# A two-layer graph kernel on one core: the last fix-up stage without its carry, products moved from GpSimd to ScalarE, and normalised rows dealt differently

## The chip, the cores and the metric

The kernel runs on one NeuronCore of one Trainium2 chip. The metric is device time in microseconds; 1742.92 us is the median of three runs of the kernel before. Engines are named as in the profile: PE is TensorE (PEld its weight loads), DVE is VectorE, ACT is ScalarE, POOL is GpSimd, SP is SyncE, which here only issues DMAs.

## What is computed

There are N = 100000 nodes with 128 features, and E = 25000 edges sorted by destination. Cut to what matters:

```python
# layer 0: attention over the edges that end in a node, then residual and layer norm
x = layernorm(x + gnn0(x, edge_attr, edge_index))
# layer 1
X1   = x @ w2
msgs = X1[src] * edge_weight[:, None]
agg  = segment_sum(msgs, dst, num_segments=N)
x    = layernorm(x + relu(x @ w1 + agg + b))
```

Only some 25000 nodes are the end of an edge. So both layers are computed twice: a dense pass over all nodes as if there were no edges, and a fix-up pass that computes the nodes with edges properly and scatters their rows over the dense ones.

## The kernel before

**Tiles.** Nodes are handled in G = 196 groups of 512 rows (128 partitions x NJ = 4 rows). Edges lie in a grid of 128 partitions x T = 196 columns, in order of destination; partition p holds edges p*196 to p*196+195. A run is a stretch of edges with the same destination. A run's sum is formed along the columns of a partition; where a run goes over from one partition to the next, the sum so far has to be carried across.

**Stages, in order of time.** (A) Dense layer 0 over 196 groups, with the gathers and the attention logits of all edges: until about 657 us. (B1) Fix-up of layer 0, 98 steps of two edge columns, scattered to `h_tab` by POOL, with the dense layer 1 of the first G1 = 49 groups between them: from about 715 to 1065 us. (D2) The dense layer 1 of groups 49 to 195: to about 1383 us. (C) Fix-up of layer 1, T4 = 49 quads of four edge columns: to the end.

**Stage D2.** For each group ACT copies the transposed rows out of PSUM (`d2_evict`, L817), PE multiplies (L619), DVE adds and takes the statistics (`d2_relu` L1238, `pair_stats` L992), ACT computes the reciprocal deviation (`inv_std`, L682 and L684), and the four rows of the group are normalised: three by ACT (`scale_rows`, L728, NZ = 3), one by DVE (`normalise`, L1002). SP loads each group ahead, ACT's queue stores it. Beside this POOL gathers the source rows of one edge column at a time from `h_tab` (L499), and four columns later multiplies them with the edge weights (L505, `agg_b2`); a gather waits for the product of six columns before. DVE forms the run sums (`run_sum`, L1228), one column after the other, some six columns behind.

**Stage C.** Per quad k: SP loads the four columns' own rows (`xg<-hd_scr`, L383); PE transposes them and the four run sums (L653, L656; signal `t_c`); ACT copies both out of PSUM (`c_evict`, L863 and L864, after `t_c` of its quad and `mm_c` of the quad two before); PE forms the product (L667, L671, L672; signal `mm_c`). DVE waits for `mm_c`, adds the carried sum `carg` to each of the four rows where the run began in an earlier partition (L1314), then normalises the quad before (L1002; signal `z_c`), then adds the residual (L1329) and takes statistics (L992). ACT's `inv_std` of quad k-3 stands ahead of its `c_evict(k)`. POOL waits for `z_c` and issues four scatters of 128 rows to the output (L514). DVE may write a buffer of normalised rows again when its scatters have landed; there are U = 4 such buffers. `carg` is made ahead of the loop: `last_sums` (L1279, L1280), two transposes (L639, L640), a scan (L1298), a product (L644), a copy (L1301).

The order of the work on each engine is the order of the program; every wait is a semaphore.

## Time and profile before

| | |
|---|---|
| median of three runs | 1742.92 us (1738.02 to 1744.43) |
| span of the profiled execution, first to last instruction | 1705.3 us |
| PE, PEld, DVE, ACT, POOL busy over the span | 73%, 64%, 79%, 72%, 61% |
| share of the chain that ended last, by engine | ACT 36%, DVE 29%, PE 9%; "another core or an unknown queue" 9%, "issue" 11% |
| HBM traffic over the span | 230 GB/s |

For the profiled execution only its span is given, no time of its own around it; the median of the runs is 37.6 us over the span. "Remote" or "another core or an unknown queue" in a row means that the profile found no releaser for the wait; on one core it is a signal whose sender the records don't show. A row of the timeline gives start, duration, engine, line, operation, tiles, count, and in brackets the idle time before it with its releaser.

### The profile page before, as it was taken

The numbers are of one execution on the slowest core, as the hardware profiler recorded it, in microseconds if no ns is written. First come the engines' busy times: TensorE is split into PE (matmuls) and PEld (weight loads), VectorE is DVE, ScalarE is ACT, GpSimd is POOL, SyncE is SP. The second block draws the span as 40 slices with busy tenths as digits, with TensorE's granted clock in tenths as the row PEclk, the third lists the DMA queues.
The fourth block names the chain that finished last, engine by engine and source line by source line (L and its number), as shares of the span: only waits on it lengthen the run. The fifth ranks groups of instructions, "written<-read, shape, count | busy, mean of one in ns | idle before, by whom it ended". The sixth has DMA issues, their size and how long they took to land.

```text
span 1705.3 us, 34722 instructions
## 1 busy us (share of the span) xinstructions
PE 1245.0 (73%) x9184; PEld 1095.8 (64%) x9184; DVE 1346.5 (79%) x5156; ACT 1225.0 (72%) x4231; POOL 1042.2 (61%) x1182
## 2 busy tenths in 40 slices
PE   1888888888888882288877876788888876665661
PEld 1877777777777772177766766666666675554551
DVE  2777898889999998888877876799999984654653
ACT  0899999999999995077787876899999962222221
POOL 2666666555566660055555656888888846666665
PEclk9999999999999996599999997999999997787876
DMA  6899999999999996734444445899999942222221
GB/s 189 269 306 302 305 305 304 303 302 301 305 301 305 308 300 233 240 117 152 154 144 140 156 141 168 270 289 292 293 289 294 292 143 77 79 82 74 86 77 38
DMA packets 210148, 372.00 MB, mean 218 GB/s; under 512 B 36740, under 2 KB 67821, under 8 KB 208935
## 3 DMA queue, kind: packets, MB, share of 16 engines
q1 hardware_dynamic: 120822, 200.48, 37.2%
q10 hardware_dynamic: 57771, 108.12, 17.3%
q0 software_dynamic: 31360, 61.17, 13.2%
q8 instruction: 77, 1.26, 0.3%
q14 instruction: 118, 0.97, 0.2%
HBM read 231.39 MB, written 161.37 MB: 230 GB/s over the span
## 4 chain that ended last, share of the span: by engine, by line
ACT 36%; DVE 29%; issue 11%; another core or an unknown queue 9%; PE 9%; DMA 1%; POOL 1%; SPq 1%; DVEq 1%; ACTq 0%; POOLq 0%
ACT hout L728 10%; ACT scan_buf L728 10%; DVE stats L992 7%; DVE hpre L1238 6%; ACT big L756 4%; ACT em L688 3%; DVE big L1228 3%; DVE hpre L1314 2%; ACT lv L769 2%; PE pd L596 2%; DVE hout L1002 2%; DVE scan_buf L1002 2%; PE pd L597 2%; PE pk L619 2%
## 5 line engine op out<-in xcount | busy, mean ns | idle before, releaser
L992 DVE BATCH_NORM_STATS2 stats<-hpre 128x6 f32<-128x256 f32 x882 | 334.8, 421 | 1.8
L466 POOL DMA_INDIRECT ring_a<-in_x,gidx x196 | 185.6, 947 | 207.4 <-PE pt L556 146.7
L728 ACT ACTIVATE scan_buf<-hpre,nb,rs 128x128 f32<-128x128 f32 x686 | 292.1, 480 | 2.8 <-DVE scan_buf L1002 1.3
L728 ACT ACTIVATE hout<-hpre,nb,rs 128x128 f32<-128x128 f32 x686 | 292.2, 480 | 2.5 <-issue 1.2
L1098 DVE SCALAR_TENSOR_TENSOR hpre<-pd,beta,xg 128x128 f32<-128x128 f32 x784 | 221.3, 345 | 29.0 <-DVE beta L1091 1.0
L565 PE MATMUL pd<-w_sx,scan_buf 128*128 128x129 f32 x1568 | 229.7, 276 | 0.0
L469 POOL DMA_INDIRECT ring_b<-in_x,gidx x196 | 185.0, 944 | 60.0 <-issue 60.0
L619 PEld LDWEIGHTS pk<-w_sb,scan_buf 128*128 128x128 f32 x1568 | 211.5, 196 | 7.4
L499 POOL DMA_INDIRECT big<-h_tab,gidx x196 | 193.4, 987 | 35.0 <-POOL big L505 29.5
L619 PE MATMUL pk<-w_sb,scan_buf 128*128 128x128 f32 x1568 | 209.9, 278 | 0.0
L565 PEld LDWEIGHTS pd<-w_sx,scan_buf 128*128 128x128 f32 x1568 | 207.0, 192 | 2.7
L483 POOL DMA_INDIRECT h_tab<-ring_a,sidx x100 | 99.7, 997 | 159.1 <-ACT ring_a L809 125.1
L562 PE MATMUL pd<-bias,ones 128*128 128x258 bf16 x392 | 107.9, 275 | 92.6 <-issue 82.7
L688 ACT ACTIVATE em<-pd,top_c 128x4 f32<-128x4 f32 (+1 forms) x294 | 77.7, 264 | 105.2 <-PE pd L597 51.5
L1314 DVE SCALAR_TENSOR_TENSOR hpre<-pair,pfar,pk 128x128 f32<-128x128 f32 x196 | 54.6, 341 | 120.6 <-remote 105.4
L514 POOL DMA_INDIRECT out_z<-hout,sidx x100 | 102.6, 1026 | 70.3 <-DVE hout L1002 42.0
L863 ACT ACTIVATE scan_buf<-pd 128x512 f32<-128x512 f32 x49 | 28.8, 589 | 147.0 <-remote 136.9
L554 PE MATMUL pt<-bias,ones 128*128 128x256 bf16 x784 | 118.5, 274 | 18.3 <-DMA r_o<-r_o 18.3
L514 POOL DMA_INDIRECT out_z<-scan_buf,sidx x96 | 97.7, 1018 | 48.0 <-issue 27.1
L616 PE MATMUL pk<-bias,ones 128*128 128x512 bf16 x196 | 78.3, 399 | 62.4 <-issue 27.4
L562 PEld LDWEIGHTS pd<-bias,ones 128*128 128x128 bf16 x392 | 38.3, 98 | 132.5 <-issue 123.5
L682 ACT ACTIVATE lv<-stats,eps_c 128x4 f32<-128x4 f32 x245 | 70.6, 288 | 72.1 <-DVE stats L992 69.2
(208 smaller groups left out, 3692.4 us busy)
## 6 DMA issues: line engine op xcount, KB each, us to landing
xg<-in_x SPq DMA_DIRECT2D x196, 256.0 KB
scan_buf<-in_xT SPq DMA_DIRECT2D x196, 256.0 KB
val<-h_tab SPq DMA_DIRECT2D x139, 256.0 KB
h_tab<-hout ACTq DMA_DIRECT2D x98, 256.0 KB
h_tab<-scan_buf ACTq DMA_DIRECT2D x98, 256.0 KB
out_z<-hout ACTq DMA_DIRECT2D x98, 256.0 KB
out_z<-scan_buf ACTq DMA_DIRECT2D x98, 256.0 KB
h_two<-h_tab SPq DMA_DIRECT2D x57, 256.0 KB, 9.1
```

The source lines that it names most:

```text
L466: gp.indirect_dma_start(out=ring_a[:, u, :], out_offset=None, in_=x[:, :], in_offset=bass.IndirectOffsetOnAxis(ap=gidx[:, k, 0:1], axis=0))\
L469: gp.indirect_dma_start(out=ring_b[:, u, :], out_offset=None, in_=x[:, :], in_offset=bass.IndirectOffsetOnAxis(ap=gidx[:, k, 1:2], axis=0))\
L499: gp.indirect_dma_start(out=agg[:, k, :], out_offset=None, in_=h_tab[:, :], in_offset=bass.IndirectOffsetOnAxis(ap=gidx[:, k, 0:1], axis=0))\
L514: gp.indirect_dma_start(out=out[:, :], out_offset=bass.IndirectOffsetOnAxis(ap=sidx[:, k:k + 1], axis=0), in_=hout[q % U][:, i * D:(i + 1) ...
L554: pe.matmul(pt[:, u % 2, 2 * P:4 * P], ones3[:, :], bias3[:, 0:2 * P], start=True, stop=True)
L562: pe.matmul(pd[:, u % 2, 2 * b:2 * b + 2, 0:D + 1], ones3[:, :], bias_x2, start=True, stop=False)
L565: mm = pe.matmul(pd[:, u % 2, j, 0:D + 1], xgT[:, u, j * P:(j + 1) * P], w_sx[:, 0:D + 1], start=False, stop=j % 2 == 1)
L619: mm = pe.matmul(pk[:, g % 2, i * D:(i + 1) * D], xgT[:, g % 2, i * P:(i + 1) * P], w1_sb[:, :], start=False, stop=i == NJ - 1)
L688: act.activation(e, logit, ACT.Relu, bias=top_c[:, 0:1], scale=sign).then_inc(cl_sem, 1)
L728: ins = act.activation(hout[ju][:, i * D:(i + 1) * D], hpre[:, ju, i * D:(i + 1) * D], ACT.Identity, bias=nb_of(ju, i), scale=rs_of(ju, i))
L992: ins = dve.bn_stats(stats[:, ju, i, :, :].rearrange("p j s -> p (j s)"), two)
L1098: ins = dve.scalar_tensor_tensor(out=hpre[:, u, i * D:(i + 1) * D], in0=pd[:, u % 2, i, 0:D], scalar=beta[:, u % 2, i:i + 1], in1=xg[:, u, ...
```

## The change

- **Carry.** The loop of stage C has no carry any more. Each quad is computed with the sum of its own partition alone: `L1314` goes, and the residual step reads PSUM directly. A partition's first run can be wrong by that; its corrected row is computed once at the end for all 128 partitions ("the x rows"): the run sums are stored to a DRAM table `agg_scr` (49 stores of 256 KB by SP), POOL gathers the last sum of the first run of each partition and its `h` row after quad 44, and after the loop PE, DVE and ACT transpose, scan, multiply, add, take statistics and normalise one tile of 128 rows, which POOL scatters last. `skip_heads` (on DVE, at group G1 + 16) works out these rows' numbers with 11 small operations and sends the wrong rows' index out of bounds.
- **Run sums.** DVE forms the first 16 columns' run sums in the last groups of D2, and the other 180 inside stage C, four quads ahead of PE, four per quad.
- **Products with the edge weight.** POOL multiplies the first 16 columns only, after all its gathers; ACT multiplies the other 180 in stage C, four per quad (`weigh_rows`). A gather waits for the landing of the gather of six columns before.
- **Ring.** The normalised rows of stage C go to ten buffers (UZ = 10) in place of four.
- **ACT's order in C.** `c_evict(k)`, four `weigh_rows`, then `inv_std` of quad k-1.
- **Dense rows.** In D2, ACT and DVE share the four rows of a group 3:1 and 2:2 by turns (`rows_act`).
- Semaphores of the setup are merged, with no change of order.

```diff
-            for k in range(T + GL):
-                if k < T:
-                    if k >= UG:
-                        gp.wait_ge(S["agg_b2"], k - UG + 1)
-                    gp.indirect_dma_start(out=agg[:, k, :], out_offset=None, in_=h_tab[:, :],
...
-                j = k - GL
-                if j >= 0:
-                    gp.wait_ge(hs_in[j % UG], 16 * (j // UG + 1))
-                    gp.tensor_tensor(agg[:, j, :], agg[:, j, :], ew_t[:, j:j + 1].to_broadcast([P, D]),
-                                     ALU.mult).then_inc(S["agg_b2"], 1)
+            for k in range(T):
+                if k >= UG:
+                    gp.wait_ge(hs_in[k % UG], 16 * (k // UG))
+                gp.indirect_dma_start(out=agg[:, k, :], out_offset=None, in_=h_tab[:, :],
...
+            for t in range(NJ * KQ):
+                gp.wait_ge(hs_in[t % UG], 16 * (t // UG + 1))
+                gp.tensor_tensor(agg[:, t, :], agg[:, t, :], ew_t[:, t:t + 1].to_broadcast([P, D]), ALU.mult)\
+                    .then_inc(S["agg_b2"], 1)
...
+            for q in range(T4 - 4):
+                scatter_quad(q)
+            gp.wait_ge(S["agg_st"], 16 * T4)
+            gp.indirect_dma_start(out=agg_x, out_offset=None, in_=agg_scr[:, :],
...
+            gp.indirect_dma_start(out=h_x, out_offset=None, in_=h_tab[:, :],
...
+            for q in range(T4 - 4, T4):
+                scatter_quad(q)
+            gp.wait_ge(S["sc"], 10)
+            gp.indirect_dma_start(out=out[:, :],
...
+        def rows_act(g):
+            return NZ - (g - G1) % 2 if g >= G1 else NZ
...
             for k in range(T4 + 1):
-                g = k - 1
                 if k < T4:
                     ku = k % U
...
                     dve.wait_ge(S["mm_c"], k + 1)
+                    dve.wait_ge(ring["hd_in"][ku], 16 * (k // U + 1))
                     if k >= U:
                         dve.wait_ge(S["z_c"], k - U + 1)
-                    for i in range(NJ):
-                        t = NJ * k + i
-                        ins = dve.scalar_tensor_tensor(out=hpre[:, ku, i * D:(i + 1) * D], in0=carg,
-                                                       scalar=psame[:, t:t + 1], in1=pk[:, k % 2, i * D:(i + 1) * D],
-                                                       op0=ALU.mult, op1=ALU.add)
-                    ins.then_inc(S["cy_c"], 1)
...
+                    dve.scalar_tensor_tensor(out=hpre[:, ku, :], in0=pk[:, k % 2, :], scalar=0.0, in1=xg[:, ku, :],
+                                             op0=ALU.max, op1=ALU.add).then_inc(S["u_c"], 1)
+                    first = NJ * (k + KQ)
+                    for t in range(first, min(first + 1, T)):
+                        run_sum(t)
                     dve.wait_ge(S["u_c"], k + 1)
                     pair_stats(ku, NJ // 2).then_inc(S["bn_c"], 1)
+                    for t in range(first + 1, min(first + NJ, T)):
+                        run_sum(t)
+                if k > 0:
+                    g = k - 1
+                    dve.wait_ge(S["rs_c"], g + 1)
+                    if g >= UZ:
+                        dve.wait_ge(z_sc[g % UZ], NJ * 16 * (g // UZ))
+                    normalise(lambda i: z_rows(g)[:, i * D:(i + 1) * D],
+                              lambda i: hpre[:, g % U, i * D:(i + 1) * D], g % U, NJ).then_inc(S["z_c"], 1)
...
+            act.wait_ge(S["agg_b2"], NJ * KQ)
+            for k in range(T4 + 1):
+                if k < T4:
+                    if 2 <= k:
+                        c_evict(k)
+                    for t in range(NJ * (k + KQ), min(NJ * (k + KQ + 1), T)):
+                        weigh_rows(t)
+                if k > 0:
+                    j = k - 1
                     inv_std(act, stats[:, j % U, :, :, 2], 1.0 / D, lv[:, j % U, :, :], rs[:, j % U, :, :],
                             S["bn_c"], S["lv_c"], S["rs_c"], j)
```

## Rows read from the trace of the kernel before

**Rows 1.** The page's first line.
```profile
span 1705.3 us, 34722 instructions
```

**Rows 2.** Busy time by stretch (PE, PEld, DVE, ACT, POOL; clock; DMA share; GB/s): A, D2.
```profile
200.00:300.00 100.00, 84.76 (x707) 76.64 (x706) 90.22 (x412) 94.21 (x356) 60.79 (x65) 1.00 0.94 305
1068.00:1323.00 255.00, 204.95 (x1540) 173.21 (x1538) 241.92 (x741) 244.40 (x711) 225.65 (x319) 0.99 0.94 288
```

**Rows 3.** Groups by line, 1068 to 1323 us: count | busy, mean ns | idle before.
```profile
L499 POOL DMA_INDIRECT big<-h_tab,gidx x162 | 159.9, 987 | 29.6 <-POOL big L505 24.1 <-DMA h_tab<-ring_a,sidx 3.5 <-issue 2.0
...
L728 ACT ACTIVATE scan_buf<-hpre,nb,rs 128x128 f32<-128x128 f32 x177 | 74.2, 483 | 0.8 <-issue 0.4
...
L505 POOL TENSOR_TENSOR big<-big,ew_t 128x128 f32<-128x128 f32 x157 | 65.8, 419 | 3.0
L1228 DVE SCALAR_TENSOR_TENSOR big<-big,same 128x128 f32<-128x128 f32 x151 | 57.3, 380 | 4.6 <-DVE big L1228 0.5
```

**Rows 4.** POOL alone from its first scatter in C to its last: stretch, busy, clock, DMA.
```profile
1397.30:1697.60 300.30, 200.31 (x196) 0.77 0.25 77
```

**Rows 5.** What POOL waited for in C: us in total, times, longest.
```profile
POOL out_z L514 <- DVE hout L1002: 42.3, 9, 18.5
POOL out_z L514 <- DVE scan_buf L1002: 20.9, 7, 5.0
```

**Rows 6.** Timeline, all engines, one standstill of C, 1414 to 1429 us.
```profile
1414.62 0.30 PE L656 MATMUL pd<-ident,big 128*128 128x128 f32 x1 [0.75 <-issue]
...
1419.59 0.60 ACT L863 ACTIVATE scan_buf<-pd 128x512 f32<-128x512 f32 x1 [9.92 <-remote]
...
1422.63 0.97 POOL L514 DMA_INDIRECT out_z<-hout,sidx  x1 [0.30 <-issue]
...
1426.02 1.12 DVE L1314 SCALAR_TENSOR_TENSOR hpre<-pair,pfar,pk 128x128 f32<-128x128 f32 x4 [9.26 <-remote]
...
1427.06 1.11 DVE L1002 TENSOR_SCALAR hout<-hpre,stats,rs 128x128 f32<-128x128 f32 x4
...
1428.09 0.68 DVE L1329 SCALAR_TENSOR_TENSOR hpre<-hpre,xg 128x512 f32<-128x512 f32 x1
1428.44 1.17 POOL L514 DMA_INDIRECT out_z<-hout,sidx  x1 [4.84 <-DVE hout L1002]
...
1428.80 0.76 DVE L992 BATCH_NORM_STATS2 stats<-hpre 128x6 f32<-128x256 f32 x2
```

**Rows 7.** Timeline of POOL and DVE in B1, 932 to 938 us.
```profile
932.67 0.97 POOL L483 DMA_INDIRECT h_tab<-own,sidx  x1 [0.30 <-issue]
...
935.16 0.69 DVE L1238 SCALAR_TENSOR_TENSOR hpre<-pk,xg 128x512 f32<-128x512 f32 x1 [4.02 <-remote]
```

**Rows 8.** Timeline at the start of A, in POOL's tenth gather in a row.
```profile
41.46 1.07 PE L565 MATMUL pd<-w_sx,scan_buf 128*128 128x129 f32 x4
41.52 0.94 POOL L469 DMA_INDIRECT ring_b<-in_x,gidx  x1 [0.30 <-issue]
...
42.56 0.26 ACT L688 ACTIVATE em<-pd,top_c 128x4 f32<-128x4 f32 x1 [3.64 <-PE pd L565]
```

**Rows 9.** Timeline of DVE from D2 to C, 1381 to 1392 us.
```profile
1383.92 2.62 DVE L1228 SCALAR_TENSOR_TENSOR big<-big,same 128x128 f32<-128x128 f32 x6
...
1390.12 0.28 DVE L1297 COPY hpre<-pt 128x128 f32<-128x128 f32 x1 [2.46 <-issue]
...
1390.44 0.42 DVE L1298 TENSOR_TENSOR_SCAN hpre<-hpre,pt 128x128 f32<-128x128 f32 x1
```

**Rows 10.** Timeline, all engines, the end.
```profile
1682.95 0.30 ACT L682 ACTIVATE lv<-stats,eps_c 128x4 f32<-128x4 f32 x1 [2.91 <-DVE stats L992]
...
1683.52 1.24 DVE L1002 TENSOR_SCALAR hout<-hpre,stats,rs 128x128 f32<-128x128 f32 x4 [0.60 <-issue]
...
1696.50 0.97 POOL L514 DMA_INDIRECT out_z<-hout,sidx  x1 [0.30 <-issue]
```

**Rows 11.** Groups by line over C, 1391 us to the end: the scatters.
```profile
L514 POOL DMA_INDIRECT out_z<-hout,sidx x100 | 102.6, 1026 | 70.3 <-DVE hout L1002 42.0 <-issue 27.9 <-DVE scan_buf L1002 0.3
```

More of the change, by code:

```diff
@@ new lines, in _ @@
+            dve.wait_ge(S["sc_pe"], 7)
+            link(dve.scalar_tensor_tensor(out=u_x, in0=pk[:, 0, 0:D], scalar=0.0, in1=h_x, op0=ALU.max, op1=ALU.add))
+            dve.bn_stats(stats_x[:, :, :].rearrange("p j s -> p (j s)"),
+                         u_x.rearrange("p (f j) -> p f j", j=1).to_broadcast([P, D, 2])).then_inc(S["sc"], 1)
+            dve.wait_ge(S["sc"], 9)
+            dve.wait_ge(S["sc_act"], 8)
+            dve.tensor_scalar(z_x, u_x, stats_x[:, 0, 1:2], rs_x[:, 0:1], ALU.subtract, ALU.mult).then_inc(S["sc"], 1)
```

239 lines of the change are left out of this document (142 added, 97 removed).

## The prediction

> **What bounds the kernel now.** I read the busy time by stretch first, because the page's averages mix four stages, then the groups by line of D2, then, for C, the waits of POOL and the timeline of one period.
>
> The profiled execution spans 1705.3 us [rows 1]; the median of the runs is 1742.92 us, 37.6 us more. I make every sum as a difference on the profiled execution and add it to the median, taking the 37.6 us as unchanged.
>
> D2 is bound by ACT: 244.4 us busy of 255, PE 205, DVE 241.9 and POOL 225.7 [rows 2]. In this stretch ACT copied 119 groups, so a group takes 255/119 = 2.14 us. The DMA engines are near their end too: 288 GB/s at a share of 0.94, where the highest rate of any long stretch is 305 GB/s at the same share [rows 2].
>
> C is not bound by any busy engine. From POOL's first scatter to its last are 300.3 us with 200.3 us busy [rows 4]. POOL's waits for DVE are 63.2 us [rows 5]; 18.5 of them lie ahead of the first scatter, so 44.7 us lie inside. The rest, 300.3 - 44.7 = 255.6 us, is 196 scatters at 1.30 us: 0.97 to 1.03 us each and 0.30 us of issue. So C's floor is POOL's issue, and 44.7 us are above it.
>
> Rows 6 show what makes the 44.7 us. PE has done the transposes of a quad by 1414.92, but ACT, which waits for their signal, goes on at 1419.59 with "remote" as releaser; DVE, waiting for the product, at 1426.02. In between POOL works off the quads that it already has, one scatter after the other, ends the last at 1423.60, and sits idle for 4.84 us [rows 6]. DVE goes on 2.4 us after POOL's last scatter was issued, about when that must have landed. This period comes nine times in the 49 quads, each time with 4.3 to 5.0 us of idle POOL; 9 x 4.84 = 43.6 of the 44.7 us. What I read from it: **when scatters have gone out back to back for some 8 us, PE's signals reach ACT and DVE late, and only after POOL has run dry do they all come through.** B1, which scatters too, has the same picture on a smaller scale: DVE stands 4.02 us and goes on 1.5 us after POOL's last scatter of the burst [rows 7]. D2, where POOL's queue gathers without a pause, has not: ACT is busy 244.4 of 255 us there [rows 2]. And at the start of A POOL issues ten gathers in a row; in the tenth ACT starts at 42.56, 0.03 us after PE's product ended [rows 8]. So scatters do it, gathers as far as the rows go do not. I can't say from the trace by what path.
>
> **The change, part by part.**
>
> *POOL's products leave D2.* A gather and a product take (159.9 + 65.8 + 29.6)/162 = 1.58 us [rows 3]; without the product a gather takes about 1.28 us, as the scatters do, so all 196 take 251 us instead of 309. POOL doesn't bound D2, so this alone gives nothing; it raises the gathers' load from 65.5 KB/1.58 us = 42 GB/s to 51 GB/s while they last.
>
> *Dense rows 3:1 and 2:2.* ACT loses half a row per group. Three rows in a chain take about 1.25 us where one takes 0.48 [rows 3], so a further row is worth 0.39 us and half a row 0.20 us: 2.14 to 1.94 us per group. DVE gains half a row (0.17 us) but loses 151/118 = 1.28 run sums of 0.38 us, 0.49 us [rows 3], so it is not next. DMA is next: the gathers take 51 of 305 GB/s, which leaves 254 GB/s for 2 x 262 KB per group, 2.06 us. For 147 groups: 251 us of gathers hold 122 groups at 2.06, the other 25 take 1.94 each, 300 us together, against 147 x 2.14 = 314.6. **-14 us.** Bounds: -29 if DMA lets ACT have its whole 0.20 us; +8 if the rate stays at the 288 GB/s of now (237 GB/s for the groups, 2.21 us).
>
> *`skip_heads`.* 11 small operations with four links on DVE, some 3 us once, queued ahead of `d2_relu` of one group; DVE has 0.3 us of slack per group to make it good. **+1 us** (0 to 3).
>
> *Start of C.* The carry's two transposes, scan, product and copies go: DVE waits 2.46 us for them and works on them until 1391.7 [rows 9]. But the first normalised quad now needs the second product and four run sums as well, each 0.44 us in a row (six took 2.62 us [rows 9]). **-1 us** (-5 to +1).
>
> *C, one quad.* DVE drops 4 carry rows (1.12 us) and takes four run sums (1.75 us); with residual 0.68, statistics 0.76 and rows 1.11 [rows 6] it needs 4.3 us per quad instead of 3.45 us, less than POOL's 5.1. ACT adds four products of 0.39 to 0.48 us to about 1.6 us: 3.3 us. Both are covered by POOL. SP's 49 extra stores of 256 KB find DMA a quarter busy [rows 4].
>
> *C, one standstill.* Here the order on DVE counts. Before, from the release to the last row of `z_c` are 1.12 + 1.11, overlapped 2.15 us [rows 6]. After, DVE does residual 0.68, one run sum 0.44, statistics 0.76, three run sums 1.31, rows 1.11: 4.30 us, and POOL, which is dry, waits for all of it. 2.15 us more, nine times: **+19 us.** Bounds: 0, if a wait elsewhere covers it; +19 as said (at the carry rows' pace of 0.28 us a run sum it is 14).
>
> *Ten buffers.* DVE never waits for the landing of the scatters of four quads before; its waits in C are for PE. So the larger ring gives **0**, as long as PE's signals are what is late.
>
> *Scatter price.* The run sums now lie beside scatters. Scatters beside the carry take 1.02 to 1.03 us [rows 11], gathers beside run sums 0.987 us [rows 3], so I take **0**; +8 if every one of 199 gets 0.04 us longer, the difference between gathers in D2 and in A (0.94 us in rows 8). Something more is rival 4.
>
> *POOL's three extra DMAs.* Two gathers and the last scatter: 3 x 1.30 = **+4 us.**
>
> *The x rows at the end.* DVE's last normalisation ends at 1684.8, POOL's last scatter at 1697.5 [rows 10]; 12.7 us of cover for a chain of signals PE to DVE (copy and scan 0.7), PE (four products, about 1.5), DVE (residual and statistics, about 0.8), ACT (two of 0.2 to 0.3), DVE (0.34): 4 us. If PE's signals came in time, the cover is enough. But they fall into the last burst of scatters, so I let the chain begin when that has landed: 2.4 + 4 = **+6 us** (0 to 8).
>
> **Sum.** -14 + 1 - 1 + 19 + 0 + 4 + 6 = +15 us, so 1742.9 + 15 = **1758 us.** Bounds of this case 1746 to 1775.
>
> **The rivals.**
> 1. *POOL never runs dry.* The late signals belong to something that the change removes (four carry reads of PSUM, a buffer ring of four), or DVE gets far enough ahead in ten buffers to carry POOL over a standstill. For it: a quad costs DVE 4.3 us and POOL 5.1. Against: the release comes each time after POOL is dry, and DVE can't get ahead while PE's signals are late. 1742.9 - 14 + 1 - 1 - 44.7 + 4 = 1688 us. Chance 0.22.
> 2. *The standstills cost what they cost now, and the end is covered.* 1742.9 - 14 + 1 - 1 + 4 = 1733 us, 1718 with D2's full 29 us. For it: the nine standstills may shift against DVE's order. Chance 0.26. This is the case that ends not slower; it holds if DVE's 2.15 us more lie under ACT or PE in the period.
> 3. *Gathers back to back do it as well.* In D2 of now every gather is parted from the next by a product; after the change they go out like the scatters for 251 us. If PE's signals then come one per 6.4 us (1419.59 to 1426.02 in rows 6) and a group needs two, 251 us hold 20 groups, the other 127 take 246 us: D2 takes 497 instead of 315 us, about 1940 us in all. Against: rows 8. Chance 0.07.
>
> 4. *Run sums hold up the scatters.* The carry rows read PSUM, a run sum reads and writes SBUF alone; if each of the 180 run sums in C stops a scatter for its own 0.44 us, POOL needs 79 us more: 1758 + 79 = 1837 us. Against: gathers beside 151 run sums take 0.987 us, against 0.94 us where there are none [rows 3, 8]; that is a tenth of it. Chance 0.02.
> The Trainium skill (SBUF — State Buffer, "SBUF: two separate sides", the box on how DVE blocks a DMA of GpSimd) has this as a rule: descriptors of such a DMA can't be written while DVE runs an operation over both of its SBUF ports. Its example is a DMA of about 620 ns that takes about 3100 ns beside a copy; the trace of D2 shows nothing of that size beside run sums.
>
> **How the numbers follow.** Forecast 0.43, rivals 0.22, 0.26, 0.07 and 0.02. About 0.5% (8.7 us) is what a measurement of this kernel can tell from no change. Faster by more: rival 1 and half of rival 2, 0.35. Within: the other half of rival 2 and 0.05 for the lower end of the forecast, 0.18. Slower: the rest of the forecast and rivals 3 and 4, 0.47. Range: from 1685, which takes in rival 1, to 1775, the forecast's upper bound; rivals 3 and 4 are left out.
>
> **What would show it.** Right: POOL's waits for DVE in C of 6 to 7 us, nine or so of them; D2 at 2.06 us per group while gathers last, with DMA at 0.95; the x rows' chain after POOL's last quad. Wrong: POOL's scatters 1.28 us apart through all of C (rival 1); DVE or ACT waiting "remote" in D2 (rival 3); D2 at 1.94 us per group (a DMA limit that I set too low); scatters well over 1.03 us (rival 4).

## The result, and the profile after

The kernel after takes 1969.28 us (median of four runs, 1964.12 to 1975.06), the kernel before 1741.24 us in the same count of runs (1738.02 to 1744.43): a ratio of 1.132, 95% interval 1.128 to 1.136. The forecast was 1758 us with a range up to 1775; it was wrong by 211 us.

The page of after: the span, the busy digits of four rows in 40 slices of 49.1 us, PE's granted clock, the DMA share and rate.

```profile
span 1964.0 us, 34556 instructions
...
PE   2888888888888327787776310012899986666563
...
DVE  2777888899899887777777200002999995455563
ACT  1899999999999617777777200002999995343341
POOL 2655565556555005555555677772000003656556
PEclk9999999999999769988898655555999997778766
DMA  6899999999999773444444522222888873333332
```

In slices 24 to 27, from 1129 to 1326 us, only POOL works. PE, DVE and ACT are at 0 or 1 tenth and DMA is at 2. That lies in the first part of D2, where POOL sends its 196 gathers (1088 to 1336 us). When the gathers have ended, all three are back at 8 or 9 tenths. By stretch (columns as in [rows 2]):

```profile
1200.00:1300.00 100.00, 9.50 (x39) 8.04 (x39) 5.08 (x16) 6.06 (x17) 75.61 (x81) 0.52 0.26 68
1400.00:1600.00 200.00, 181.19 (x1384) 154.46 (x1382) 188.51 (x588) 196.62 (x587) 0.00 (x0) 1.00 0.88 279
```

In [rows 2] ACT was busy 244 of 255 us beside the gathers; now it is 6 of 100. Without gathers it is 197 of 200, and a group then takes 1.88 us (117 groups from 1380 to 1600 us), near the 1.94 of the forecast. The granted clock of PE is 0.52 in the first stretch, its lower level (1.2 GHz) nearly throughout; it fell to it at 1112 us, inside the first stretch of 30 us in which PE stood idle (1108.8 to 1138.7). This is no cause, since PE's matmuls fill a tenth of the time. Who waits for what from 1060 us on (total, times, longest):

```profile
POOL out_z L550 <- DVE val L1071: 352.2, 16, 282.2
ACT scan_buf L871 <- remote: 254.9, 10, 34.6
DVE hpre L1307 <- remote: 187.0, 7, 34.8
```

The releaser is "remote", as in C's standstills [rows 6], but a wait is 34 us in place of 9. The gathers themselves, between 1080 and 1336 us, are nearly as forecast (1.28 us): 1.25 us apart, against 1.58 us before [rows 3].

```profile
L535 POOL DMA_INDIRECT big<-h_tab,gidx x196 | 187.9, 958 | 64.5 <-issue 64.5
```

One cycle of this, from the timeline (POOL and small rows left out):

```profile
1163.37 0.69 DVE L1307 SCALAR_TENSOR_TENSOR hpre<-pk,val 128x512 f32<-128x512 f32 x1 [34.77 <-remote]
...
1174.40 0.60 ACT L871 ACTIVATE scan_buf<-pt 128x512 f32<-128x512 f32 x1 [34.22 <-remote]
...
1175.06 0.61 PE L668 MATMUL pk<-bias,ones 128*128 128x512 bf16 x1 [33.23 <-issue]
1175.46 1.91 PE L671 MATMUL pk<-w_sb,scan_buf 128*128 128x128 f32 x8
1177.17 1.06 PE L661 MATMUL pt<-ident,val 128*128 128x128 f32 x4
...
1199.77 0.69 DVE L1307 SCALAR_TENSOR_TENSOR hpre<-pk,val 128x512 f32<-128x512 f32 x1 [34.46 <-issue]
```

By the trace PE has done the product by 1177.2 and the transposes by 1178.2 (the ends of matmuls are modelled in it). DVE, which waits for the product, goes on at 1199.8; ACT, which waits for the transposes, at 1210.8. Groups come at 1163.37, 1199.77, 1236.20, 1272.60 and 1309.00, 36.4 us apart.

Where the two profiled executions differ, by the start of POOL's first and last DMA of each stage:

| stage | before, us | after, us | difference |
|---|---|---|---|
| start to D2's first gather (no work moved) | 1068.2 | 1088.4 | +20.2 |
| D2, first gather to C's first scatter | 329.1 | 549.2 | +220.1 |
| C, first to last of the 196 scatters | 299.2 | 320.3 | +21.1 |
| the rest | 8.8 | 6.1 | -2.7 |
| span | 1705.3 | 1964.0 | +258.7 |

The 20.2 us ahead of D2 belong to no part of the change: before_without_products, one of the kernels below, has the code of before up to there and sends D2's first gather at 1094.5 us. In all later executions a span lies some 2 us under its time, so the profiled execution of before took about 1707 us. It was a quick one, as before is in one session below (1702 to 1721 us), and its 37.6 us to the median did not lie around the span, as I had taken them to.

### The profile page after: what moved, and what is told of

It is laid out like the page before. It is cut to its first block, busy times and chain, and to the rows that moved or that the text cites. A ratio compares the mean times of both kernels' runs of the same rounds, so it can differ in the third digit from the quotient of the medians.

```text
span 1964.0 us, 34556 instructions
## 1 busy us (share of the span) xinstructions
PE 1277.0 (65%) x9191; PEld 1126.5 (57%) x9191; DVE 1309.4 (67%) x5045; ACT 1252.1 (64%) x4342; POOL 955.2 (49%) x1006
## 4 chain that ended last, share of the span: by engine, by line
ACT 33%; DVE 21%; another core or an unknown queue 16%; issue 14%; PE 12%; DMA 1%; POOL 1%; DVEq 0%; SPq 0%; ACTq 0%; POOLq 0%
ACT scan_buf L782 9%; ACT hout L782 9%; DVE stats L1061 4%; DVE hpre L1167 3%; ACT scan_buf L871 3%; PE pd L648 3%; ACT big L810 3%; PE pd L649 2%; ACT em L742 2%; PE pk L671 2%; DVE big L1297 2%; DVE val L1071 2%; ACT lv L736 1%; DVE val L1113 1%
## 5 line engine op out<-in xcount | busy, mean ns | idle before, releaser
L550 POOL DMA_INDIRECT out_z<-val,sidx x196 | 192.5, 982 | 408.4 <-DVE val L1071 352.2
L782 ACT ACTIVATE scan_buf<-hpre,nb,rs 128x128 f32<-128x128 f32 x649 | 279.5, 485 | 2.8 <-DVE scan_buf L1071 2.7
L782 ACT ACTIVATE hout<-hpre,nb,rs 128x128 f32<-128x128 f32 x650 | 279.9, 484 | 2.2 <-DVE hout L1071 1.8
L871 ACT ACTIVATE scan_buf<-pt 128x512 f32<-128x512 f32 x196 | 113.9, 581 | 260.3 <-remote 255.4
L1307 DVE SCALAR_TENSOR_TENSOR hpre<-pk,val 128x512 f32<-128x512 f32 x147 | 100.8, 685 | 268.3 <-remote 187.0
L671 PEld LDWEIGHTS pk<-w_sb,scan_buf 128*128 128x128 f32 x1568 | 223.0, 205 | 8.6
L671 PE MATMUL pk<-w_sb,scan_buf 128*128 128x128 f32 x1568 | 221.1, 287 | 0.0
L535 POOL DMA_INDIRECT big<-h_tab,gidx x196 | 187.9, 958 | 64.5 <-issue 64.5
L668 PEld LDWEIGHTS pk<-bias,ones 128*128 128x128 bf16 x196 | 19.6, 100 | 305.3 <-issue 176.8
L1383 DVE SCALAR_TENSOR_TENSOR hpre<-pk,xg 128x512 f32<-128x512 f32 x49 | 33.8, 690 | 141.1 <-remote 117.8
```

The lines of the kernel that those rows point to most:

```text
L535: gp.indirect_dma_start(out=agg[:, k, :], out_offset=None, in_=h_tab[:, :], in_offset=bass.IndirectOffsetOnAxis(ap=gidx[:, k, 0:1], axis=0))\
L550: gp.indirect_dma_start(out=out[:, :], out_offset=bass.IndirectOffsetOnAxis(ap=sidx[:, k:k + 1], axis=0), in_=z_rows(q)[:, i * D:(i + 1) * ...
L671: mm = pe.matmul(pk[:, g % 2, i * D:(i + 1) * D], xgT[:, g % 2, i * P:(i + 1) * P], w1_sb[:, :], start=False, stop=i == NJ - 1)
L782: ins = act.activation(hout[ju][:, i * D:(i + 1) * D], hpre[:, ju, i * D:(i + 1) * D], ACT.Identity, bias=nb_of(ju, i), scale=rs_of(ju, i))
L871: act.activation(xgT[:, g % 2, :], pt[:, bank_of(g), :], ACT.Copy).then_inc(S["hT_d2"], 1)
```

## The experiments

The kernels were measured in five sessions, each on one chip (the expectations say "call"), and the kernel before ran beside the others in each. It took 1737, 1746, 1711 and 1741 us in four sessions and 1572 us in one; every ratio below is within its session. A kernel for which no interval is given ran once. The 13 runs of before in the session of 1711 us lie between 1702 and 1721 us, so single runs tell nothing about differences of that size.

The expectations weigh theories that go by letters. **O:** another part of the change holds up D2. **S:** an indirect DMA that follows the last one with no other instruction of POOL between them holds up PE's signals. **R:** the mean rate of POOL's DMAs counts. **M:** one signal comes through per so many DMAs. **L:** while the DMAs follow one another with too little idle time between them, one instruction of PE completes per DMA.

### Which part it is

**One part alone.** The kernel before without POOL's products:

```diff
-            for k in range(T + GL):
+            for k in range(T):
...
-                        gp.wait_ge(S["agg_b2"], k - UG + 1)
+                        gp.wait_ge(hs_in[k % UG], 16 * (k // UG))
...
-                    gp.tensor_tensor(agg[:, j, :], agg[:, j, :], ew_t[:, j:j + 1].to_broadcast([P, D]),
-                                     ALU.mult).then_inc(S["agg_b2"], 1)
...
-                dve.wait_ge(S["agg_b2"], t + 1)
+                dve.wait_ge(hs_in[t % UG], 16 * (t // UG + 1))
```

> The kernel before with one part of the change alone: POOL's 196 products are left out (the messages are not weighted, that part of the computation is missing), so that its gathers follow one another; each waits for the landing of the gather six before, and DVE's run sums wait for the landing. Theories S and R: the gathers are 1.25 to 1.28 us apart, groups of D2 take about 36 us while they last, D2 takes about 250 us more: about 1950 to 1980 us. Theory O: 1741 us or less.

Measured: 1974.29 us beside 1737.14. Its waits from 1060 to 1500 us:

```profile
DVE hpre L1233 <- remote: 218.0, 8, 34.5
ACT scan_buf L812 <- remote: 216.4, 8, 34.9
```

The same 34.5 us as in after. Nothing else of the change is in this kernel (the gather's wait for a landing instead of the product comes with it), so the products' leaving POOL is enough by itself.

**The same part undone.** The kernel after, with the products back between the gathers and ACT's products gone from C:

```diff
+                j = k - 4
+                if j >= 0:
+                    gp.wait_ge(hs_in[j % UG], 16 * (j // UG + 1))
+                    gp.tensor_tensor(agg[:, j, :], agg[:, j, :], ew_t[:, j:j + 1].to_broadcast([P, D]), ALU.mult)\
+                        .then_inc(S["agg_b2"], 1)
...
-                    for t in range(NJ * (k + KQ), min(NJ * (k + KQ + 1), T)):
-                        weigh_rows(t)
```

> The kernel after, with the products on POOL between the gathers of D2 again, as before, and ACT's four products per quad gone from C; nothing is left out. Theories S and R both expect D2 at about 290 to 310 us and the whole at 1690 to 1740 us. Theory O expects 1950 to 1970 us.

Measured: 1737.07 us beside 1737.14. The loss of D2 is gone, and with it some 230 us. D2 from its first gather to C's first scatter is 313.4 us (329.1 before), and at its end it is POOL that is late:

```profile
1381.76 0.67 DVE L1310 SCALAR_TENSOR_TENSOR hpre<-pk,val 128x512 f32<-128x512 f32 x1
...
1400.08 1.05 POOL L535 DMA_INDIRECT big<-h_tab,gidx  x1 [0.16 <-issue]
...
1403.60 0.40 POOL L545 TENSOR_TENSOR big<-big,ew_t 128x128 f32<-128x128 f32 x1 [0.83 <-DMA big<-h_tab,gidx]
1404.54 1.02 POOL L555 DMA_INDIRECT out_z<-val,sidx  x1 [0.54 <-issue]
```

DVE starts D2's last group at 1381.76; POOL sends its last gather at 1400.08, does the last product, and C's first scatter follows. The dense groups take 2.00 us each (147 starts in 291.5 us) against 2.16 before, which is some 24 us less, but only 16 of them shorten the stage. C takes 324.8 us. In the same session before_without_products, whose C is that of before, has 303.6 us (the trace of before has 299.2), so the rest of the change loses about 21 us in C.

### What it depends on

**A small instruction in between.**

```diff
+            def gap(n=1):
...
+                gp.memset(ring_b[:, 3, m % 64:m % 64 + 1], 0.0).then_inc(S["gap"], 1)
...
                     .then_inc(hs_in[k % UG], 16)
+                gap()
```

> The kernel after, with one memset of 128x1 on POOL after each of the 196 gathers of D2; nothing is left out. Theory S (an indirect DMA that follows the last one with no other POOL instruction between them holds up PE's signals): DVE and ACT no longer wait 34.5 us per group; D2 falls from 554 us to about 290 us (147 groups at 1.88 to 2.06 us), the whole from 1969 to about 1705 us. Theory R (the rate of gathers counts: 1.25 us apart here, 1.58 us in the kernel before): the memset adds perhaps 0.1 to 0.2 us, the gathers stay closer than 1.5 us, and the groups of D2 still take over 20 us each while they last: 1940 us or more. Theory O (another part of the change holds up D2): 1969 us.

Measured: 1954.03 us beside 1737.14. Two groups by line and one wait of D2, 1110 to 1370 us:

```profile
L543 POOL DMA_INDIRECT big<-h_tab,gidx x180 | 170.0, 945 | 59.9 <-issue 59.4
L537 POOL MEMSET ring_b<- 128x1 f32 x180 | 20.8, 115 | 5.6 <-issue 4.5 <-remote 1.0
...
DVE hpre L1316 <- remote: 206.6, 12, 27.5
```

The memset lies inside the 0.30 us that POOL idled anyway, the median spacing stays 1.25 us, and the waits stay at up to 27 us. D2 up to C's first scatter still takes 541 us, where theory S had some 290; that another instruction must stand in between falls. The memset is not without effect, though. Groups start every 18 us in place of 36.4, and the mean spacing is 1.41 us: after some ten gathers in a row POOL itself pauses for a few, with spacings up to 2.8 us. What makes it pause no run shows.

**Spaced by a wait alone.**

```diff
-                if k >= UG:
-                    gp.wait_ge(hs_in[k % UG], 16 * (k // UG))
+                if k >= 2:
+                    gp.wait_ge(hs_in[(k - 2) % UG], 16 * ((k - 2) // UG + 1))
```

> The kernel after, where a gather of D2 waits for the landing of the gather two before it (in place of six before): POOL executes no other instruction between two gathers, but they are spaced by a wait, about 1.6 us apart or more. Theory S in its strict form (an instruction of another kind must stand between) expects D2 to stay near 550 us and the whole at 1969 us or more. If idle time on POOL or a lower rate is enough (theory R, or theory S with a pause in place of an instruction), D2 is about 300 to 330 us and the whole about 1710 to 1750 us.

Measured: 1858.38 us. D2 between 1100 and 1300 us, and POOL's gathers there:

```profile
1100.00:1300.00 200.00, 176.88 (x1354) 151.14 (x1353) 184.87 (x581) 192.15 (x573) 75.92 (x80) 1.00 0.93 304
...
L535 POOL DMA_INDIRECT big<-h_tab,gidx x80 | 75.9, 949 | 126.2 <-DMA big<-h_tab,gidx 117.0 <-issue 9.2
```

ACT is busy 192 of 200 us with no instruction between the gathers, so none has to stand there; more time between them is enough. The spacing is uneven here, 1.25 to 4.5 us, and fewer gathers are under way at once. Whether it is the time between two DMAs or the number under way that counts, this kernel doesn't part, nor do the others. The kernel is late for another reason: a gather per 2.0 us takes 389 us in all, and the first products and run sums wait for that (139 us once).

**How much spacing.** A product of w columns that nothing uses after each gather, w falling every 28 gathers:

```diff
+            def pad(w, n=1):
...
+                    gp.tensor_tensor(ring_b[:, 2 + m % 2, 0:w], ident[:, 0:w],
+                                     ew_t[:, 0:1].to_broadcast([P, w]), ALU.mult).then_inc(S["gap"], 1)
...
+                w = (128, 96, 64, 48, 32, 16, 0)[k // 28]
+                if w:
+                    pad(w)
```

> The kernel after, with a 128 x w product of POOL after each gather of D2 that nothing uses: w is 128 for the first 28 gathers, then 96, 64, 48, 32, 16 for 28 each, and none for the last 28. To be read by section: the spacing of the gathers, and the time of a group. Theory L expects a bound on idle time between two DMAs: normal groups (1.9 to 2.1 us) at w = 128, where the spacing is 1.58 us, and at the widths down to some limit; below that, 10 to 36 us per group. Theory R (the mean rate alone counts) expects a smooth rise, with half of the lateness at half of the spacing's difference, near w = 64. The whole: 1800 us, between 1730 and 1900.

Measured: 1874.36 us. By section, from the starts of the gathers and of DVE's first instruction of a group; the last column is the number of PE instructions of a group, 26, times the spacing over the time of a group:

| w | spacing, us | groups | us per group | PE instructions per gather |
|---|---|---|---|---|
| 128 | 1.592 | 21 | 2.12 | 19.5 (not late) |
| 96 | 1.521 | 16 | 2.66 | 15 |
| 64 | 1.472 | 10 | 4.12 | 9 |
| 48 | 1.449 | 7 | 5.80 | 6.5 |
| 32 | 1.414 | 5 | 7.92 | 4.6 |
| 16 | 1.391 | 3 | 13.0 | 2.8 |
| none | 1.250 | 1 | 35.0 | 0.9 |

Three stretches of it, w = 128, 48 and 16, as the profile has them:

```profile
1105.00:1140.00 35.00, 29.08 (x222) 24.82 (x223) 33.81 (x106) 31.95 (x95) 30.96 (x45) 1.00 0.92 294
1230.00:1265.00 35.00, 14.90 (x70) 12.65 (x71) 10.85 (x33) 11.69 (x33) 30.71 (x49) 0.69 0.44 135
1310.00:1345.00 35.00, 6.33 (x26) 5.35 (x26) 3.63 (x11) 3.89 (x11) 29.59 (x47) 0.50 0.27 78
```

The last rows rest on few groups. Between 1.39 and 1.52 us the last column rises by 12 for 0.13 us: it is a steep rise with no step, and it lies between the spacing of after and that of before. Theory R had half of the loss gone near w = 64; of the 33 us per group 31 are gone there.

**Pauses between bursts.**

```diff
+                every, n = ((2, 1), (4, 1), (4, 2), (8, 2), (8, 4))[min(k // 40, 4)]
+                if k % every == every - 1:
+                    pad(128, n)
```

> The kernel after, with 128 x 128 products of POOL that nothing uses after every second gather of D2 (first 40 gathers), one after every fourth (next 40), two after every fourth (next 40), two after every eighth (next 40), four after every eighth (last 36). Theory L: if a pause lets only one more PE instruction complete, all sections are as slow as after's (20 to 36 us per group); if the backlog goes in any pause of some 0.5 us, groups take 1.9 to 2.5 us in the first section and at most the length of a burst plus 1 us, 6 and 11 us, in the others. Theory R: every second at 1.42 us and two after every fourth at 1.46 us behave alike.

Measured: 1945.87 us. With one pad after every second gather ten groups start in the section's 56.5 us, 5.6 us each. In the next three sections it is 27, 20 and 27 us per group, in the last one group starts in 50 us; they hold three groups at most. Every second gather has a mean spacing of 1.41 us, two pads after every fourth 1.42 us in the regular pattern (1.49 with one gap of 4.6 us), and theory R had these two alike. They are 5.6 and 20 us, so the mean rate is not the rule: a longer pause gives back less than the same pause split up. A long pause doesn't clear D2's backlog either.

### What comes late: each instruction of PE

```diff
-                                   w1_sb[:, :], start=False, stop=i == NJ - 1)
+                                   w1_sb[:, :], start=False, stop=i == NJ - 1 and g < G1)
+                if g >= G1:
+                    for i in range(NJ):
+                        mm = pe.matmul(pk[:, g % 2, i * D:(i + 1) * D], xgT[:, g % 2, i * P:(i + 1) * P],
+                                       w1_sb[:, :], start=False, stop=i == NJ - 1)
```

> The kernel after, where PE does the four products of each group of D2 a second time into the same sum (so the product with w1 counts double there, and that part of the output is another). In the trace of after one group's product is 18 PE instructions (nine loads, nine matmuls) and its signal comes 22.6 us after its end, the transposes are 8 more and their signal comes 32.6 us after their end, with gathers 1.255 us apart: 18.0 and 26.0 gathers. Theory L (while POOL's indirect DMAs follow one another, one PE instruction completes per DMA, so lateness goes by the number of PE instructions): 16 more instructions, 20.1 us more per group while the gathers last, 36.4 becomes 56.5 us, and DVE's waits 54 us. Theory M (one signal comes through per so many gathers, whatever lies behind it): 36.4 us per group as in after.

Measured: 2045.70 us beside 1746.38. Groups come at 1193.06, 1251.86 and 1310.66, 58.8 us apart, where one signal per so many gathers would have left 36.4. So the number of PE's instructions counts. The law had one detail wrong: not one per gather of 1.25 us, but 58.8/42 = 1.400 us for each, and in after 36.4/26 = 1.400 us too. In this kernel it can be seen on PE itself, since 42 instructions are more than it runs ahead. Timeline, PE and its weight loads:

```profile
1213.18 0.29 PEld L675 LDWEIGHTS pk<-w_sb,scan_buf 128*128 128x128 f32 x1 [2.50 <-issue]
1214.58 0.37 PE L675 MATMUL pk<-w_sb,scan_buf 128*128 128x128 f32 x1 [2.43 <-issue]
1215.28 0.29 PEld L675 LDWEIGHTS pk<-w_sb,scan_buf 128*128 128x128 f32 x1 [1.81 <-issue]
1216.68 0.37 PE L675 MATMUL pk<-w_sb,scan_buf 128*128 128x128 f32 x1 [1.73 <-issue]
1218.09 0.28 PEld L675 LDWEIGHTS pk<-w_sb,scan_buf 128*128 128x128 f32 x1 [2.52 <-issue]
1219.48 0.37 PE L675 MATMUL pk<-w_sb,scan_buf 128*128 128x128 f32 x1 [2.43 <-issue]
```

One load or one matmul, in turn, each 1.40 us (one pair is closer), where the work of one is 0.3 us. The first 22 instructions of the group start within 2.4 us; after that one starts per 1.40 us, as if PE got a new one only when an old one completes.

### Stage C

**Pads in C**, on the kernel products_back, by sections of quads:

> The run products_back (the kernel after with POOL's products back between the gathers of D2) with products of POOL that nothing uses between the scatters of C: none in quads 0 to 11; 128x128 after each scatter in quads 12 to 21; 128x32 after each in quads 22 to 31; one 128x128 per quad, after its fourth scatter, in quads 32 to 41; none in the rest. If the standstills of C come from scatters that follow one another (theory L), they are gone in quads 12 to 21, which then take 6.3 us each (four times 1.58 us), and in the two other sections they are gone or fewer, with 5.6 to 6.0 us per quad where they are gone. If they come from something else (DVE's or PE's work in C), quads 12 to 21 take 6.3 us plus the 1.2 us of standstill that a quad bears in products_back. Whole: 1725 to 1750 us.

Measured: 1719.64 us beside 1746.38. From the first to the last scatter 305.0 us, where products_back has 324.8. Quads 0 to 11 take 6.30 us each and have 3 waits of POOL over 2.5 us; quads 12 to 21 (w = 128) 6.62 and none; quads 22 to 31 (w = 32) 5.92 and none; quads 32 to 41 (one pad per quad) 5.44 and none until, ahead of quad 42, POOL waits 7.0 us. PE was busy only 22 us in the 59 us of that section: POOL lived on the ten buffers filled before.

**The order on DVE.** products_back, and the same with the run sums behind the normalisation:

```diff
-                    for t in range(first, min(first + 1, T)):
-                        run_sum(t)
                     dve.wait_ge(S["u_c"], k + 1)
                     pair_stats(ku, NJ // 2).then_inc(S["bn_c"], 1)
-                    for t in range(first + 1, min(first + NJ, T)):
-                        run_sum(t)
...
+                if k < T4:
+                    for t in range(first, min(first + NJ, T)):
+                        run_sum(t)
```

> The kernel products_back, unchanged, for an interval. Where before takes 1740 us: 1737 us, no difference from before. Where before takes 1572 us: no standstills, so D2's 14 us are kept: 1550 to 1570 us.

> products_back, with DVE's four run sums of a quad moved behind the normalisation of the quad before (in place of one ahead of the statistics and three ahead of the normalisation). Where before takes 1740 us: if the order on DVE makes a standstill longer, as the prediction had it (four run sums of 0.44 us ahead of the rows POOL waits for), each of the 13 gets 1.7 us shorter and the kernel takes some 20 us less than products_back; if POOL's idle time is set by when PE's signals come, no difference. Where before takes 1572 us: no difference either way.

Measured, in one session: products_back 1710.01 us, ratio 0.999 (0.995 to 1.003); with the sums last 1690.57 us, 0.987 (0.982 to 0.993). POOL's waits in C, first of products_back, then with the sums last, and under them one release of DVE with POOL's next scatter, again of the one and of the other:

```profile
POOL out_z L555 <- DVE val L1074: 70.8, 11, 7.0
```

```profile
POOL out_z L555 <- DVE val L1074: 49.2, 14, 4.7
```

```profile
1521.27 0.69 DVE L1386 SCALAR_TENSOR_TENSOR hpre<-pk,xg 128x512 f32<-128x512 f32 x1 [10.17 <-remote]
...
1525.56 0.97 POOL L555 DMA_INDIRECT out_z<-val,sidx  x1 [6.84 <-DVE val L1074]
```

```profile
1510.24 0.69 DVE L1386 SCALAR_TENSOR_TENSOR hpre<-pk,xg 128x512 f32<-128x512 f32 x1 [7.64 <-remote]
...
1513.02 0.97 POOL L555 DMA_INDIRECT out_z<-val,sidx  x1 [4.46 <-DVE val L1074]
```

From DVE's release to POOL's scatter are 4.29 us with the run sums ahead and 2.78 behind; before it was 2.42 [rows 6]. The standstills themselves stay, and C is 303.6 us in place of 322.4.

**Spacing in place of order.** products_back with `pad(32)` after each scatter of C:

> The kernel c_padded, unchanged: products_back with a 128x32 product of POOL after each of C's scatters. Where before takes 1740 us, theory L expects standstills gone or rare, C about 290 us in place of 325, and 1700 us, 2% below before; if the spacing of 1.45 us isn't enough there, 1715 to 1735 us. Where before takes 1572 us the pads are only a price: 1585 us, as in the last call.

Measured: 1680.64 us, ratio 0.982 (0.977 to 0.988). C is 291.0 us. POOL in C, by line:

```profile
L567 POOL DMA_INDIRECT out_z<-val,sidx x189 | 193.0, 1021 | 31.2 <-issue 31.2
L524 POOL TENSOR_TENSOR spare<-ident,ew_t 128x32 f32<-128x32 f32 x190 | 50.2, 264 | 5.5
```

It doesn't wait for DVE at all any more. The scatters are 1.455 us apart, 0.18 us each is the price, some 35 us in all, and 70.8 us of waits are what it buys; C is 31.4 us shorter than in products_back of the same session.

**B1, and A.** The last kernel with the pad in B1 too and the sums last, and the same with the pad in A:

> products_back with a 128x32 product of POOL that nothing uses after each scatter of B1 and of C, and with DVE's run sums of C behind the normalisation. Beside a kernel before of 1710 to 1745 us: C as in c_padded_2, 291 us (the order on DVE is worth nothing once there are no standstills; ratio 0.982 by that alone). B1 took 328 us there from its first scatter to its last and 276 us on the chip where PE's signals were never late. If B1's 52 us are late signals too, and spacing its scatters ends them, B1 takes 280 to 300 us and the kernel 30 to 45 us less: ratio 0.955 to 0.965. If B1's loss has another cause, 0.98 to 0.985. Beside a kernel before of 1570 us: 1590 us, ratio 1.013.

> The same, and the pad also after each of A's 392 gathers, which go out four in a row. A took 400 us for 129 groups, 3.10 us each (200 to 600 us in the trace of the kernel before), and 2.93 us on the chip where signals were never late; ACT's waits for late signals are short there (54 of 0.3 us). If the spacing frees PE's signals in A, up to 0.17 x 196 = 33 us less than b1_c_padded_sums_last. If not, POOL needs 2 x 1.43 = 2.9 us per group, under 3.10: no difference, within 5 us.

Measured, in one session: 1683.80 us, ratio 0.969 (0.966 to 0.973), and 1688.05 us, 0.972 (0.968 to 0.975). The first is the fastest of all against the kernel before. C is 294 us with the sums last and 291 in c_padded_2 with the sums ahead, so the order is worth nothing once there are no standstills. From B1's first scatter to its last are 323 us. No kernel without B1's pads ran beside these two. Such kernels have 347 us where before took 1737 us and 347 to 353 where it took 1746, near the 1741 here, but 331 where it took 1711. The 24 us to 347 and the ratio, 1.3% under c_padded_2's, agree on some 20 us for B1's pads; across sessions that is an estimate, and the 280 to 300 us of the expectation were not reached. In A the pads win nothing: the gathers go from first to last in 620 us, 614 without pads.

### A session without late signals

> The kernel before, unchanged, in one more profiled execution. The profiled execution that the prediction was read from spans 1705.3 us, while the spans of other executions of the same kernel lie about 2 us under their times of 1737 to 1746 us. If it was merely a quick one, this execution spans about 1735 to 1742 us, and the comparison of the two traces shows where the 30 us lie: spread over A, B1, D2 and C alike (about 2% each), or in one stage. If 37 us lie around the span, this execution's time is 37 us over its span.

> products_back, with a 128x32 product of POOL that nothing uses after each of C's 196 scatters. In pad_c ten quads with this pad took 5.92 us each with no standstill, but with ten buffers filled by the section before. Theory L: scatters 1.45 to 1.5 us apart all through C, no wait of POOL over 1 us but at the start, C about 49 x 5.9 = 290 us in place of 325, the whole about 1700 us. If the ten quads lived on the filled buffers, PE's instructions are still too late at this spacing, standstills come back, and C takes 6.2 to 6.6 us per quad: 1715 to 1735 us.

> c_padded, with the same pad of 128x32 also after each of B1's 196 scatters. Theory L: B1's standstills (DVE waiting 4 us for PE, some 41 us of such waits in all in products_back) go as well, POOL has idle time there to pay for the pads; B1 takes 10 to 30 us less, and the whole is that much below c_padded. If B1 is bound by PE's and ACT's own work, no difference.

> The kernel before, with a 128x32 product of POOL that nothing uses after each of C's scatters, and nothing of the change. C had nine standstills of 4.84 us, 300 us in all, 6.1 us per quad. Theory L: the standstills go, a quad takes 4 x 1.48 = 5.9 us, C 290 us, the whole 8 to 12 us less than before. With only four buffers the standstills may come back in part: then 0 to 10 us more than before.

These four ran in one session. The kernel before took 1571.64 us there (1570.79 for before_again), c_padded 1585.27 us, ratio 1.011 (1.006 to 1.015), b1_c_padded 1589.92 us, 1.013 (1.004 to 1.022), before_c_padded 1602.73 us. The page of before_again, and its POOL in C:

```profile
span 1569.2 us, 34722 instructions
...
POOL 0766666666666663017666766888888885777776
PEclk9999999999999999579999998999999999889985
```

```profile
POOL out_z L514 <- issue: 59.1, 194, 0.3
POOL out_z L514 <- DVE hout L1002: 13.7, 2, 13.4
```

The scatters follow one another, 1.28 us apart in the median, with no wait but the 13.4 us ahead of the first. The same program needs 256.1 us from first scatter to last here and 299.2 in the trace of before. The difference, 43 us, is the nine standstills of [rows 6] nearly to the microsecond. B1 takes 275.6 us in place of 334.3, A's groups 2.94 us in place of 3.12 (136 and 128 of them in 400 us); D2, whose gathers are 1.58 us apart in both, takes 324.5 against 329.1. The pads are then a price only: C 289 us in place of 256. What made the session without late signals different I can't say: its chip has the same number as that of an earlier session in which before took 1737 us, so a property of the chip alone is unlikely. Whether after is fast in such a session was not found out: after_again was meant for it and met signals as late as ever.

One more thing differs between the traces, and it bears on all of this. A trace also holds a record of each change of a semaphore. Of the same program, with all its 34722 instructions in both, before_again holds 43374 such records and the trace of before 15958. The traces of c_padded, b1_c_padded and before_c_padded hold 43606 to 44650, the 16 traces with late signals 15285 to 18356. The landings of D2's 196 gathers should raise six semaphores 16 times each, 3136 times in all: before_again has 3105 of these records, before 1204, after 336. While the gathers follow one another in after (1110 to 1330 us), its trace keeps 1.4 records per us, where the gathers alone make 12.8; without gathers (1400 to 1600 us) it keeps 21.8, and before_again beside its gathers (1000 to 1260 us) 30.2.

So signals are late in the sessions in which records are missing, and most are missing where signals are latest; that is also in keeping with the releaser "remote". Either the recording holds back PE, or both suffer from the same thing. No run can part the two, because every execution on record, the timed ones too, comes with a recorded span and clock. All times here are those of recorded executions; whether PE's signals are late in one that is not recorded stays open.

> The kernel after, unchanged. The last four kernels ran in a call in which the kernel before took 1572 us, not 1737 to 1746, and its trace had no late signal of PE at all: no wait of POOL over 2.5 us in C, scatters 1.28 us apart, 256 us from the first scatter to the last in place of 299. So the lateness belongs to the chip that a call gets, not to the program alone. If this call is like that one (before near 1572 us), the same gathers, 1.25 us apart, hold up nothing: D2 at 1.9 to 2.1 us per group, C's scatters 1.28 us apart, and after is at 1540 to 1570 us, at or below before. If PE's signals come late there too when gathers follow one another, 1790 us or more. If this call is like the earlier ones (before near 1740 us): 1969 us again.

Measured: 1946.42 us beside 1710.91, ratio 1.135 (1.128 to 1.143), D2 546.7 us, C 323.3 us.

## Why the prediction was wrong, point by point

- **"So scatters do it, gathers as far as the rows go do not."** This step failed, and with it the forecast and its 0.07 for rival 3: D2 was put at -14 us and came out at +220. It rested on two rows. [rows 2] shows D2 undisturbed, but at 1.58 us per gather, and pad_widths shows that this is just outside the lateness while 1.25 us is deep inside. [rows 8] shows ten gathers in a row, but that is a burst of 12 us at the very start, when PE had hardly begun. In after, too, DVE still starts a group at 1099.43, 11 us after D2's first gather, and only the next one is late, at 1126.91. What differed between C and D2 before was the spacing, 1.28 against 1.58 us, and I read the direction of the transfer out of it. I had written down the new spacing, 1.28 us, and had not compared it with C's.
- **Rival 3's mechanism was right and its size off.** It took one signal per 6.4 us, two per group, 12.5 us per group, and 1940 us. What counts is not the signal but the instructions of PE behind it, 1.40 us each: 26 of them make 36.4 us (before_without_products, product_twice). D2 came to 549 us, not 497.
- **C's standstills, +19 us.** C took 21.1 us more in after, and about 21 in products_back beside before_without_products, where the DVE order is that of after. The price for one was right: 4.29 us from release to scatter where 4.30 was worked out, and 18.8 us won in C by sums_last. That there would be nine of them was not quite: POOL waits for DVE 15 times for 70.0 us in after's C.
- **D2's own 14 us.** Right in size. In products_back D2 is 313.4 us against 329.1, 16 us less, start of C included, and in the session without late signals c_padded has 310.7 us against 322.4 in before_c_padded, 12 less. The terms were a little too dear: a group beside the gathers takes 2.00 us, not 2.06, with DMA at 309 GB/s where I had taken 305 as the end, and in after 1.88 us behind the gathers, where I had 1.94. With the products on POOL its gathers end last, and part of the gain is lost.
- **Scatter price 0, and rival 4.** The scatters of after take 982 ns, less than in [rows 11]. Run sums beside them hold up nothing. The Trainium skill's rule on how DVE blocks a DMA of GpSimd (SBUF — State Buffer, "SBUF: two separate sides") doesn't show in a single scatter here: the longest of after's 196 takes 1.08 us.
- **Ten buffers 0.** Right for after, where DVE waits for PE. In c_padded_2 POOL is the bound and the ring fills up: DVE waits 50.1 us for landings, without cost. Four against ten buffers in the same kernel was not tried; without late signals the padded C takes 288.5 us with four (before_c_padded) and 289.2 with ten (c_padded).
- **Three more DMAs +4, x rows +6.** The three take 1.0 us and 0.3 of issue each, 4 us as said. The x rows cost nothing more, where I had 6 us: they are normalised at 1950.8 us, and POOL comes to their scatter at 1959.2 with 0.3 us of issue ahead of it, so 8.4 us of the cover were left.
- **The base.** 37.6 us do not lie around the span. A sum of differences isn't moved by it, but the stage by stage comparison is: 20 us appear ahead of D2 where the work is the same.
- **What would show it** named the right sign: "DVE or ACT waiting remote in D2 (rival 3)". The range left it out.

What stays open is the path. A DMA of POOL is busy for 0.95 us in the profile, and PE's completions flow freely only from a spacing of 1.5 to 1.6 us on, so something after that busy time counts too. The Trainium skill (Perfetto Trace Analysis, "DMA Instruction — SWDGE (GPSIMD)") says that such an instruction ends in the profile when its descriptors are written, not when the data has moved; two_in_flight agrees, where a gather waits up to 4.5 us for the landing of the one two before. That the descriptors or the landing share a path with PE's completions is argued, not shown. The missing semaphore records are a second candidate: what PE's instructions wait for may be their own records. The runs show which part of the change sets the lateness off and how it goes with the spacing, not what PE waits for.

## What to carry to other kernels

Before you take an instruction out from between two indirect DMAs of GpSimd, or lay many of them back to back beside TensorE, look at their spacing: in the executions here it was what let TensorE's signals through. When waits for TensorE grow to several microseconds and end as GpSimd runs dry, space the DMAs by a small product (here 128x32, to about 1.45 us), and move whatever GpSimd doesn't wait for behind what it does. A clean stretch in the trace clears a pattern only at the spacing and the length at which it ran, so compare both before you call a rival unlikely. And when waits end with no releaser, count the semaphore records of the trace against what the program must make: where most are missing, what you read may be an effect of the recording.

## What the runs showed of the hardware that I had not expected

- In the executions of all sessions but one, while gathers of POOL go out every 1.25 us, PE gets through one instruction per 1.400 us, loads and matmuls alike (36.4 us for 26, 58.8 us for 42), and runs some two dozen ahead of that. At 1.39 us it is about 2.8 per gather, at 1.45 us 6.5, at 1.52 us 15.
- Scatters hold up PE's signals too: standstills of 4.8 us at 1.28 us apart, none at 1.455 us. The law per instruction was measured with gathers only.
- The traces with late signals hold 15000 to 18000 semaphore records, those without them 43000 to 45000, of nearly the same program.
- It need not happen: in one session the same kernel ran 10% faster, 1572 in place of 1741 us, and 194 scatters 1.28 us apart held up nothing.
